# A new table of turns for two interleaved streams of one decoder megakernel

## What is computed

```python
x = ln(x + mamba(x))                     # DI 512, 16 states, scan over 256 tokens
x = ln(x + latent_xattn(x, ctx, idx))    # 16 heads of 16, keys picked by idx (64 per query)
x = ln(x + ffn(x))                       # 256 -> 1024 -> 256, inputs fake-quantised, gelu
x = ln(x + self_attn(x))                 # 16 heads of 16
x = ln(x + cross_attn(x, ctx))           # 16 heads of 64
x = ln(x + moe(x))                       # 8 experts, top 6, and a shared one
```

## Time and profile before

| | us |
|---|---|
| median of 3 runs | 3802.04 (3790.84 to 3803.64) |
| profiled execution | 3786.92 |
| its span, first to last instruction | 3785.1 |
| DVE busy | 2833.4 (75%) |
| PE busy | 3170.1 (84%) |
| ACT busy | 2083.7 (55%) |
| POOL busy | 922.6 (24%) |

### The profile page before, as it was taken

How to read it: one execution, slowest core, us unless ns; L and a number is a source line. 1 busy time by engine, 2 the same in 40 slices (tenths; PEclk the granted TensorE clock), 3 DMA queues, 4 the chain that set the end, 5 groups by cost and what they waited for, 6 DMA issues and landing times.

```text
span 3785.1 us, 59632 instructions
## 1 busy us (share of the span) xinstructions
PE 3170.1 (84%) x22658; PEld 2253.3 (60%) x22658; DVE 2833.4 (75%) x4915; ACT 2083.7 (55%) x4816; POOL 922.6 (24%) x740
## 2 busy tenths in 40 slices
PE   2568988898898989889898998889889888988877
PEld 1345656666565666656566665666656566665655
DVE  4687786868778687877868778786877868687622
ACT  3356656565665656566464655656566565556432
POOL 1423050221404122140411305031230503114000
PEclk8689999999999999999998999999999999999988
DMA  5212141422304142130413214041331404133110
GB/s 190 81 62 94 32 142 45 147 71 80 129 21 154 52 138 80 56 129 33 166 52 130 88 43 141 34 161 57 116 102 32 153 34 155 62 104 107 48 42 17
DMA packets 208286, 338.71 MB, mean 89 GB/s; under 512 B 24480, under 2 KB 177568, under 8 KB 193280
## 3 DMA queue, kind: packets, MB, share of 16 engines
q1 hardware_dynamic: 208000, 334.90, 25.9%
HBM read 311.75 MB, written 20.97 MB: 88 GB/s over the span
## 4 chain that ended last, share of the span: by engine, by line
PE 49%; DVE 28%; ACT 15%; issue 6%; POOL 0%; SPq 0%; DMA 0%; DVEq 0%; ACTq 0%
PE ps L636 5%; PE ps L888 5%; DVE nm L1567 4%; PE ps L617 4%; PE ps L949 4%; PE ps L803 3%; PE ps L789 3%; PE ps L779 3%; ACT ps L1070 2%; PE ps L834 2%; PE ps L648 2%; DVE region_x L1544 2%; ACT region_y L1219 2%; PE ps L556 2%; DVE region_x L1524 2%
## 5 line engine op out<-in xcount | busy, mean ns | idle before, releaser
L1331 POOL TENSOR_TENSOR region_x<-region_x 128x512 f32<-128x512 f32 x512 | 646.4, 1274 | 357.7 <-DVE region_x L1544 356.5
L1544 DVE TENSOR_TENSOR_SCAN region_x<-ps,region_x 128x512 f32<-128x512 f32 x512 | 614.9, 1214 | 72.7 <-ACT ps L1070 72.3
L1070 ACT ACTIVATE ps<-region_x,aneg 128x255 f32<-128x255 f32 x1024 | 440.0, 474 | 332.7 <-DVE region_x L1544 329.5
L1311 POOL TENSOR_TENSOR region_x<-region_x 128x512 f32<-128x512 f32 x96 | 121.7, 1268 | 1184.0 <-ACT region_x L1018 1179.0
L1323 POOL TENSOR_TENSOR region_x<-region_x 128x512 f32<-128x512 f32 x128 | 162.7, 1271 | 1003.7 <-DVE region_x L1524 861.7
L1567 DVE TENSOR_REDUCE nm<-ps 128x4 f32<-128x1024 f32 x256 | 305.6, 1220 | 62.6 <-PE ps L617 58.8
L888 PE MATMUL ps<-xTy,wide 128*128 128x256 f32 x1280 | 316.5, 397 | 1.4 <-DVE region_y L1731 1.4
L1219 ACT ACTIVATE region_y<-ps,rmax 128x256 f32<-128x256 f32 x512 | 235.8, 496 | 119.1 <-DVE rmax L1672 119.1
L888 PEld LDWEIGHTS ps<-xTy,wide 128*128 128x128 f32 x1280 | 244.2, 197 | 36.1 <-DVE region_y L1731 1.6
L1672 DVE TENSOR_REDUCE rmax<-ps 128x4 f32<-128x1024 f32 x128 | 152.3, 1221 | 147.4 <-PE ps L815 147.4
L1524 DVE TENSOR_TENSOR region_x<-region_x,ps 128x512 f32<-128x512 f32 x384 | 255.7, 666 | 3.8 <-PE ps L556 3.3
(11 more groups left out here) (251 smaller groups left out, 6924.9 us busy)
## 6 DMA issues: line engine op xcount, KB each, us to landing
region_x<-rows_of_dt SPq DMA_DIRECT2D x1024, 128.0 KB, 2.8
wide<-in_wgate SPq DMA_DIRECT2D x16, 1280.0 KB, 8.2
wide<-in_wup SPq DMA_DIRECT2D x16, 1280.0 KB, 10.9
down<-in_wmoe SPq DMA_DIRECT2D x16, 1280.0 KB, 7.0
wide<-in_wq SPq DMA_DIRECT2D x16, 1024.0 KB, 5.4
wide<-in_wk SPq DMA_DIRECT2D x16, 1024.0 KB, 7.5
wide<-in_wv SPq DMA_DIRECT2D x16, 1024.0 KB, 9.6
down<-in_wo SPq DMA_DIRECT2D x16, 1024.0 KB, 12.6
```

Of the source, the lines that this page charges most:

```text
L1070: last = f(ps[:, 1 + 2 * (k % 2), half * T + 1:(half + 1) * T], dt_rep[k % SLOTS][:, 1:T], ACT.Exp, scale=aneg[:, k, half:half + 1])
L1331: nc.gpsimd.tensor_tensor(hbuf[k % HSLOTS], hbuf[k % HSLOTS], csb, ALU.mult).then_inc(hc_ready, 1)
L1544: nc.vector.tensor_tensor_scan(flat(hbuf[k % HSLOTS]), ps[:, 1 + 2 * (k % 2), :], flat(hbuf[k % HSLOTS]), 0.0, ALU.mult, ALU.add).then_inc ...
```

## The change

No instruction is added or taken away; the four entries of `ORDER` are other numbers.

```diff
-    "sp": (123, "x19 y2 x2 y1 x25 y2 x2 y1 x23"),
-    "pe": (60, "x1 y3 x1 y11 x1 y4 x1 y6 x1 y4 x1 y9 x1 y7 x2 y3 x3 y2 x1 y2 x3 y1 x1 y1 x4 y1 x1 y2 x1 y1 x2 y1 x1 "
...
-    "act": (80, "y1 x7 y1 x5 y2 x1 y1 x1 y1 x1 y2 x1 y2 x1 y3 x2 y3 x1 y3 x1 y1 x1 y2 x1 y2 x2 y3 x2 y1 x1 y3 x2 y1 "
...
-    "v": (141, "y1 x3 y1 x2 y1 x1 y6 x1 y1 x20 y1 x5 y1 x4 y1 x15 y2 x2 y4 x1 y1 x2 y1 x2 y1 x12 y1 x20 y2 x1 y1 x1 "
...
+    "sp": (142, "y3 x25 y1 x1 y2 x45"),
+    "pe": (61, "y3 x1 y11 x1 y4 x1 y6 x1 y5 x1 y9 x1 y6 x2 y3 x3 y2 x1 y2 x3 y1 x1 y1 x4 y1 x1 y2 x1 y1 x2 y1 x1 "
...
+    "act": (83, "y1 x6 y1 x3 y1 x1 y3 x1 y1 x1 y1 x1 y1 x1 y3 x1 y1 x1 y6 x1 y1 x2 y1 x1 y3 x1 y2 x1 y1 x2 y1 x1 "
...
+    "v": (142, "y1 x5 y1 x1 y7 x1 y1 x19 y1 x2 y1 x1 y1 x21 y2 x2 y4 x2 y1 x1 y1 x2 y1 x11 y1 x20 y2 x2 y1 x1 y4 "
...
```

## The result

| | before | after |
|---|---|---|
| median, one chip, four runs each (us) | 3796.44 | 3704.36 (3691.54 to 3707.49) |
| ratio | | 0.9751 [0.9732, 0.9771] |
| profiled execution (us) | 3786.92 | 3701.36 |
| DVE busy (us, share) | 2833.4 (75%) | 2772.8 (75%) |

The changed kernel is 92 us faster, where 50 were forecast, and it lies under the low end of the range. The two profiled executions differ by 86 us.

What follows compares the result with a forecast made beforehand. The prediction took a chain of waits over PE, DVE and ACT as the bound, with DVE bounding junction and scan. Terms -3.4 + 0.3 - 0.5 = -3.6 us a period, times 14 = 50 us, gave 3752 us; range 3722 to 3800.

Steps and rivals of the forecast that it cites:

- What bounds the kernel: Whole period of 222.2 us: a chain of waits over PE, DVE and ACT, read place by place from idle time.
- Down weights, 0 us: Down weights' load (L417) on SP, issued about 30 us earlier before the stores of dt: alone 0 us.
- Term A: Junction and self attention's scan: 5.26 us of DVE idle against 1.9 new, -3.4 us a period, bounds -4.8 and -0.4.
- DVE then never waits for L888: Junction: with PE's one-hot groups before DVE's third and fourth products, the 1.45 us wait before L1727 goes.
- Term B: Self attention's sum, two units earlier on DVE: +0.3 us a period, from 0 to 1.
- Term C: End of latent attention up to the router: -0.5 us a period, with -1.5 and +1.6 as ends, depending on L869.
- Fourteen junctions, fill and drain the same: Whole run: fourteen junctions with both streams gain 3.6 us each, 50 us; fill and drain cost the same.
- the clock: Rival: PE's low clock after idle holds on through self attention's key and value projections; gain 0.6 a period, 3794 us, chance 0.16.
- All is gained: Rival: junction gains 4.0 and latent attention's end 1.5 us a period, 73 us in all, 3729 us; chance 0.17.

Runs made afterwards that it cites:

- e4: Kernel before with only SP's table as after, the down weights' load ahead of the stores of dt: 3793.42 us, ratio 0.9994.
- e5: Changed kernel with SP's order of before, so the down weights' load is queued where it was: 3694.62 us, ratio 0.9734.
- e11: Kernel before with only self attention's half of the junction, scans ahead of the row maxima on DVE and ACT's copies for them: 3800.13 us, ratio 1.0023.
- e13: Kernel before with the junction's other half alone, MoE and ffn pieces on PE and DVE and ACT's turns as changed, maxima as before: 3734.23 us, ratio 0.9832.
- e10: Kernel before with only the pieces from self attention's weighing to its sum in their new turns on DVE, ACT and PE: 3790.69 us, ratio 1.0001.
- e8: Kernel before with GpSimd's second half of the convolution sums (L1311) cut to 8 of 256 columns, measuring time only: 3779.13 us, ratio 0.9959.
- e2: Kernel before with only the end of the latent attention and the start of the ffn laid out as after: 3777.10 us, ratio 0.9947.
- e6: Changed kernel with the row maxima on DVE and the two pieces on ACT as before: 3724.86 us, ratio 0.9815.

## Why the prediction was right in direction and too small

Three steps of the sum failed: the row maxima of two attentions were put at nothing, L869's slow half was given a price that it did not have, and the small step L1407 on DVE was taken for unchanged. The rest of the working held, though not in every period.

- **What bounds the kernel**: right. The gain came where DVE's idle was read off one by one.
- **Down weights, 0 us**: right, in the old order (e4) and the new (e5). The time to spare was less than the 1 or 2 us of the prediction: in the period that it reads, the load landed 8.6 us after its issue at 1579.02, near 1587.6, and L949 started at 1587.95. L428 held up no instruction of DVE or PE.
- **Term A, -3.4**: measured -3.81, and 55 us for the junction alone. The waits are mostly those forecast (L500 1.07 for 1.2, L1477 0.49 for 0.5, L1575 0.53 for 0.5, none before L1421; two L949 from 1554.48 to 1564.88, 10.4 for about 10.8). "DVE then never waits for L888" holds in eight periods of fourteen only; in the other six the wait is 1.69 to 2.04 us. The part of its working on self attention, which let three products and two scans pay for the 0.29 and 1.57, earned nothing of its own (e11, e13). What the term left out is L1407: 1.12 us before and 0.16 after, where the working kept it as it was. With the 0.18 by which L1405 is longer, that is 0.8 us a period, 11 us.
- **Term B, +0.3**: measured 0 (e10), -0.15 in its stage. A and B together are 0.86 better than forecast, 12 us in 14 periods, about what L1407 gives.
- **The missing term, -0.97**: the exchange of the row maxima of two attentions. The diff had it on one line of DVE's order, and the trace of before had the wait that it removes, 0.94 us before L1672. The prediction set the junction and the latent attention's end and took the stage between them, which moves by one instruction, for unchanged. 0.97 x 14 = 14 us. The prediction gave no reason for the nothing.
- **Term C, -0.5**: the mechanism was right in the rows shown, the size was not: -1.22 at L678 and -0.51 in the last stage, -1.73 together (its end was -1.5, for L869 at 3.67 us). The failed step is the price given to L869: the prediction let the gain go for the periods in which it takes 5.36 us, as if these would stay. Two things were wrong with that. Before the change the last stage takes 17.37 to 17.38 us in each of the first thirteen periods, whether L869 takes 5.36 or 3.67: DVE is the bound there, and the slow product costs nothing. And afterwards L869 takes 3.69 in every period, so that there was nothing to pay for. That a slow L869 costs its 1.69 us in full where PE is the bound, as the prediction had it, is shown by e8 (17.21 and 15.52); and a slow stretch on L848 costs 1.63 where it occurs (e2, e6). 1.23 x 14 = 17 us missed.
- **Fourteen junctions, fill and drain the same**: nearly. From the first router to the fifteenth the changed kernel needs 83.1 us less, 5.94 for each of 14 periods and not 6.66: the last period is 0.5 us longer than before, since DVE then waits 11.11 us for L707 before L1608 instead of 4.82.
- **The sum of what was missed**: 12 + 14 + 17 = 43 us, beside the 42 between 50 and the 92 of the medians. That they agree so closely is partly luck: the last period takes some 7 us back, and the two profiled executions differ by 86 us and not by 92.
- **Rivals**: the clock did not take the gain. It has its price in both kernels: a slow L888 adds some 1.7 us to the first stage in most of its six periods after the change, and some 2.2 us in its five before. The first L754 is slow in more periods than before (its mean product took 495 ns over the run, 465 before, 6.4 us in all), but the level does not hold on: L754 of the keys stays at 3.62. PE's time at 1.2 GHz altogether fell from 407 to 349 us of the profiled span. "All is gained" (3729) was nearest, and still too small, since it held no term for the maxima.

## What to carry to other kernels

Read more than one period before a wait is called gone or new: the one shown first here was the exception. Where an order changes, list every place in which a row moved, however little, and look up the idle time in front of each moved instruction before calling a stage unchanged. A slow stretch of an engine is a cost only where that engine is the bound: compare the length of the stage in periods with and without the stretch first. Halves of a reordering that were laid out together should be tried apart only with the turns of all engines in mind, since one engine's new turns can be a loss without the other's. And when busy time falls although no instruction went, look up which instructions became shorter, and what ran beside them.
